# A deformable convolution's last tap summed on VectorE, and a new order of the engines' steps

## What is computed

```python
for oy in (0.0, 1.0):
    for ox in (0.0, 1.0):
        yy, xx = (y0 + oy, x0 + ox)
        wgt = (1.0 - jnp.abs(ys - yy)) * (1.0 - jnp.abs(xs - xx))
        ...
        out = out + jnp.where(valid, wgt, 0.0)[..., None] * g
...
return jnp.einsum('npkgc,npkg->npgc', out, mk)
...
d = _dcn_core(v, off, mask) @ op_w.T
z = d @ cv2_w.T
```

## Time and profile before

| | us |
|---|---|
| median of 3 runs | 918.97 (918.94 to 920.76) |
| profiled execution | 918.25 |
| its span, first to last instruction | 916.4 |
| sampling, first product to last row sum | 52.9 to 421.9 |
| attention, first gather to last scatter | 622.6 to 772.7 |

### The profile page before, as it was taken

How to read it: one execution, slowest core, us unless ns; L and a number is a source line. 1 busy time by engine, 2 the same in 40 slices (tenths; PEclk the granted TensorE clock), 3 DMA queues, 4 the chain that set the end, 5 groups by cost and what they waited for, 6 DMA issues and landing times.

```text
span 916.4 us, 10354 instructions
## 1 busy us (share of the span) xinstructions
PE 599.2 (65%) x3032; PEld 446.3 (49%) x3032; DVE 538.9 (59%) x1018; ACT 322.0 (35%) x536; POOL 465.7 (51%) x364
## 2 busy tenths in 40 slices
PE   1566878787878787761288888873867771656511
PEld 0445556565656565640265665652656661445300
DVE  3257878797969796962366566552564654444411
ACT  2435352525252525100154554551232320433400
POOL 0058988899989998996100000004575733000075
PEclk9967575758585858555599999986686875677755
DMA  9463526565556562600445455410010101445311
GB/s 359 145 151 80 144 58 150 167 146 171 142 163 151 168 145 68 151 0 23 153 129 160 151 159 171 147 45 15 12 30 23 30 15 33 128 129 138 100 33 37
DMA packets 67013, 101.22 MB, mean 110 GB/s; under 512 B 25742, under 2 KB 45198, under 8 KB 66958
## 3 DMA queue, kind: packets, MB, share of 16 engines
q1 hardware_dynamic: 62416, 93.07, 35.7%
q0 software_dynamic: 4096, 6.30, 2.6%
q10 hardware_dynamic: 446, 1.20, 0.4%
HBM read 37.67 MB, written 25.10 MB: 68 GB/s over the span
## 4 chain that ended last, share of the span: by engine, by line
PE 32%; DVE 19%; issue 18%; POOL 13%; ACT 9%; SPq 5%; DMA 4%; POOLq 0%; DVEq 0%; ACTq 0%
DVE sb_prod L1085 6%; POOL sb_yg L1382 5%; POOL xs L1363 5%; PE ps_pa L479 4%; PE ps_t L514 4%; PE ps_c L472 3%; PE ps_t L581 2%; PE ps_pb L599 2%; DVE sb_hats L1160 2%; DVE sb_hats L1071 2%; ACT sb_hats L859 2%; PE ps_t L582 1%; PE ps_t L590 1%; PE ps_t L589 1%; PE ps_c L499 1%
## 5 line engine op out<-in xcount | busy, mean ns | idle before, releaser
L1351 POOL TENSOR_TENSOR sb_acc<-sb_acc,sb_prod 128x1024 f32<-128x1024 f32 x128 | 300.2, 2376 | 12.0 <-DVE sb_prod L1085 11.7
L1382 POOL DMA_INDIRECT sb_yg<-ys,sb_jdx x64 | 61.4, 959 | 295.3 <-DMA ys<-sb_yt 277.3
L514 PE MATMUL ps_t<-sb_vbd,sb_hx 128*128 128x256 f32 x576 | 139.9, 391 | 69.9 <-DVE sb_prod L1085 57.8
L1085 DVE TENSOR_TENSOR sb_prod<-ps_t,sb_hy 128x1024 f32<-128x1024 f32 x128 | 153.6, 1216 | 41.7 <-PE ps_t L514 31.9
L514 PEld LDWEIGHTS ps_t<-sb_vbd,sb_hx 128*128 128x128 f32 x576 | 110.1, 267 | 100.2 <-DVE sb_prod L1085 70.1
L1363 POOL DMA_INDIRECT xs<-sb_xr,sb_idx x64 | 64.4, 1007 | 25.4 <-issue 15.8
L1213 DVE TENSOR_TENSOR sb_hid<-ps_t,sb_hid 114x512 f32<-114x512 f32 x69 | 46.4, 686 | 46.3 <-ACT sb_hid L880 41.0
L499 PE MATMUL ps_c<-sb_dwT,sb_omx 128*128 128x256 f32 x144 | 53.5, 527 | 14.8 <-DVE sb_hats L1071 10.2
L880 ACT ACTIVATE sb_hid<-ps_t 114x512 f32<-114x512 f32 x69 | 41.2, 599 | 48.0 <-PE ps_t L582 47.9
L499 PEld LDWEIGHTS ps_c<-sb_dwT,sb_omx 128*128 128x128 f32 x144 | 34.9, 259 | 23.3 <-issue 17.4
L479 PE MATMUL ps_pa<-sb_ypad,sb_diag 128*64 128x256 f32 x96 | 40.8, 599 | 8.2 <-ACT sb_yrep L781 8.2
(11 more groups left out here) (253 smaller groups left out, 1294.2 us busy)
## 6 DMA issues: line engine op xcount, KB each, us to landing
sb_hx<-sb_hats SPq DMA_DIRECT2D x384, 96.0 KB, 2.2
xs<-sb_x3t SPq DMA_DIRECT2D x32, 512.0 KB, 6.1
sb_acc<-in_wcat SPq DMA_DIRECT2D x16, 876.0 KB, 4.5
sb_yrep<-in_wcat SPq DMA_DIRECT2D x7, 876.0 KB, 4.5
sb_nt<-xs SPq DMA_DIRECT2D x32, 128.0 KB, 2.1
sb_acc<-in_ucat SPq DMA_DIRECT2D x22, 160.0 KB, 2.4
sb_xt<-xs SPq DMA_DIRECT2D x23, 128.0 KB, 2.2
ys<-sb_yt SPq DMA_DIRECT2D x16, 128.0 KB, 2.4
```

The source lines that it names most:

```text
L514: last = mm(tb[u % 2][:, j * 256:(j + 1) * 256], hx[q % 3][:, j, o:o + P], vbd[n % 2][:, j * 256:(j + 1) * 256], start=True, stop=True)
L1085: v.tensor_tensor(o.rearrange("p (g c q) -> p g c q", g=G, q=H), tb[u % 2][:, :].rearrange("p (g c q) -> p g c q", g=G, q=H), w, ALU.mult) ...
L1351: g.tensor_tensor(acc[n % 2][:, t, :], acc[n % 2][:, t, :], prod[a % 3][:, :], ALU.add).then_inc(s_pool_acc, 1)
L1382: g.indirect_dma_start(out=yg[b][:, t, z, :], out_offset=None, in_=ys[0:NJT[m] * TILE, :], in_offset=bass.IndirectOffsetOnAxis(ap=jdx[m][: ...
```

## The change

The ninth tap (k = 8) is no longer added by GpSimd. VectorE makes its product as before, and right behind it sums that buffer over the 16 rows into a new tile `dlast` (one reduction for each half of the pixels). GpSimd adds taps 1 to 7: 14 adds per image. `sampled` on TensorE no longer transposes `dsum`; it multiplies `dsum` and `dlast` by the identity into the same PSUM region, two accumulating products for each half. The buffers' counts follow: `added` says how many adds must be done before a buffer is free. TensorE now waits for `s_dve_last` too. All five strings of `WEAVE` differ.

```diff
-ADDS = UNITS - TT
+ADDS = UNITS - 2 * TT
...
+        dlast = sb("dlast", [P, TT, C])
...
             def sampled(n):
                 pe.wait_ge(s_dve_dr, n + 1)
+                pe.wait_ge(s_dve_last, n + 1)
                 if n:
                     pe.wait_ge(s_dve_rk[0], 2 * n)
-                to_channels(pb, dsum).then_inc(s_pe_dt, 1)
+                for t in range(TT):
+                    mm(pb[0:C, t * P:(t + 1) * P], dsum[:, t, :], ident[:, :], start=True, stop=False)
+                    last = mm(pb[0:C, t * P:(t + 1) * P], dlast[:, t, :], ident[:, :], start=False, stop=True)
+                last.then_inc(s_pe_dt, 1)
...
+            def added(a):
+                n, i = divmod(a, UNITS - TT)
+                return ADDS * n + min(i + 1, ADDS)
+
             def tap(n, k, t):
                 u = UNITS * n + k * TT + t
-                a = ADDS * n + (k - 1) * TT + t
+                a = (UNITS - TT) * n + (k - 1) * TT + t
...
-                        dve.wait_ge(s_pool_acc, a - 2)
+                        dve.wait_ge(s_pool_acc, added(a - 3))
...
+                if k == K - 1:
+                    dve.wait_ge(s_dve_p, u + 1)
+                    if n:
+                        dve.wait_ge(s_pe_dt, n)
+                    last = v.tensor_reduce(dlast[:, t, :], o.rearrange("p (c r) -> p c r", r=H), AX, ALU.add)
+                    if t == TT - 1:
+                        last.then_inc(s_dve_last, 1)
...
             def tap(n, k, t):
-                if k == 0:
+                if k in (0, K - 1):
                     return
...
-                g.tensor_tensor(acc[n % 2][:, t, :], acc[n % 2][:, t, :], prod[a % 3][:, :], ALU.add).then_inc(s_pool_acc, 1)
+                g.tensor_tensor(acc[n % 2][:, t, :], acc[n % 2][:, t, :], prod[(a + TT * n) % 3][:, :], ALU.add).then_inc(s_pool_acc, 1)
...
-        zzzzzzzzaa aaaapaaazz paaazzpaaa zzpaaazzpp ppaaaaaaxx xxxdxdxdxd xdxdxdxdxd xdxdxdxdxd xdxdxdxdxd xddddxxxxx dxxddxdxxx
+        zzzzzzzzaa aaaapaaapz zaaapzzaaa pzzaaapppp zzaaaaaaxx xxxdxdxdxd xdxdxdxdxd xdxdxdxdxd xdxdxdxdxd xddddxxxxx dxxddxdxxx
```

33 lines of the change are left out of this document (17 added, 16 removed).

## The result

The changed kernel takes **953.8 us** (median of 4 runs, 950.4 to 954.8), the kernel before in the same comparison 919.9 us (918.9 to 921.5): ratio 1.0359, 95% interval 1.0335 to 1.0383, slower by 34 us. The forecast was 930.5 us, range 904 to 942. The direction was right, the size was not, and the time lies above the range.

The account below looks back on a forecast made before the run. It took GpSimd's adds and TensorE's convolution chain with VectorE behind it as about equally late. From 918.25 us, +5.6 (sampling), -4.6 (stage end), +10.6 (attention) and 0.7 to the median gave 930.5 us, range 904 to 942.

Parts of the forecast that it names:

- part 1: Sampling stage, GpSimd: two adds fewer, 4.7 us an image; its loop of about 43.3 us would allow a 2.6 us gain.
- rival A: Sampling stage: GpSimd keeps the pace, so the period falls to 43.3 us; 906.8 us, 12 in 100.
- part 2: Sampling stage, VectorE: two reductions of 1.21 us add 2.4 us an image, with no wait for their product.
- part 3: Sampling stage: VectorE idles 7.0 us against 8.3, period 46.65 us, 0.8 us more per image, +5.6 us in all.
- The two waits at the core: Sampling stage, VectorE: waits on TensorE for the transposed x1, 3.6 us, and for the logits, 2.9 us.
- part 4: Sampling stage, TensorE: four joining products replace two transposes, +0.7 to +1.6 us an image, taken as covered and charged 0.
- the slow bound: Sampling stage: upper bound of 48.0 us for the period, with all TensorE work at the lower clock.
- part 5: End of the sampling stage: two late GpSimd adds of 2.31 us go, -4.6 us.
- part 6: Attention stage's new order: one more scatter left after the gathers (63.0 us), 17.0 us of GpSimd waits among them; +10.6 us.
- B: Sampling stage: TensorE's high clock from the start of depthwise, period 44.6 us; 915.9 us, 14 in 100.
- C: Attention stage: the new order costs nothing, GpSimd's waiting among the gathers stays at 6.4 us; 920 us, 12 in 100.
- E: Sampling stage: TensorE's low clock throughout, period 48.0 us, and attention +14.6 us; 943.6 us, 9 in 100.

Follow-up runs that it names:

- relief_only: Kernel before in its order, with 14 GpSimd adds an image, the ninth tap left out of the sum and two transposes kept; 915.0 us, ratio 0.9951.
- new_order_relief: Changed kernel with the attention order of before, without ninth-tap row sums, two transposes instead of joining products; 916.7 us, ratio 0.9973 to the kernel before.
- last_only: Kernel before in its order, with the changed ninth-tap work in the last image alone (126 adds instead of 128); 913.6 us, ratio 0.9939.
- code_old_order: Changed kernel's work with the whole order of steps of the kernel before; 929.7 us, ratio 1.0118 to the kernel before.
- early_slots: early_rank with VectorE's slot sum and ScalarE's slot copy of images 2 to 4 also ahead of key maxima and exponentials; 957.2 us.
- late_scatter: old_attention with GpSimd's scatter descriptors of images 0 to 3 moved behind the hits of the next image; 933.0 us.
- early_rank: Changed kernel with TensorE's rank products of images 2 to 4 moved earlier and VectorE's rank ahead of the key maxima; 958.9 us.
- combined: old_attention with x1 ahead of depthwise products, z and column products behind a tap, and GpSimd's scatter behind the next image's hits; 925.7 us.
- x1_first: old_attention with x1's transposes ahead of the depthwise products for images 1 to 4, its dependent steps and logits moved up; 925.4 us.
- early_x1: Kernel before with summed-tap transposes, z, x1 and its norm moved earlier for images 1 to 5; 930.1 us, ratio 1.0109.
- old_attention: Changed kernel with the attention stage's order of before, sampling order as changed; 935.5 us, ratio 1.0171 to the kernel before.

## Why the prediction went wrong

- **GpSimd's relief (part 1)**: its price was right (4.7 us of GpSimd's time a period forecast, 4.5 measured) and so was that VectorE with its waits was the later of the two. relief_only shows that the relief gives nothing in the period. The 43.3 us of rival A came in neither order.
- **Reductions (part 2)**: priced at 2.42 us a period, 2.2 measured over the regular images. That they stand on the path was right: VectorE's work adds to the period nearly one to one.
- **VectorE's idle time (part 3), the step that failed most.** The two waits at the core were forecast at 3.6 and 2.9 us and are 4.49 and 2.10, together 6.6 against 6.5: the sum is right by luck, since the two errors cancel. The third term, "some 0.5 us" ahead of the third tap, is 0.46 + 1.07 + 1.02 = 2.55 us in three places: z, then the norm's transposes with the `cv1` product, then the last column products with the transposes of x stand between taps. The first of them was priced right; the other two had no term. And the busy time was summed from durations at their old places: the copy (+1.20) and the mask (+0.66) grew since adds of GpSimd now stand beside them. 46.65 + 2.05 (short waits) + 1.9 (longer operations) + 0.1 (core waits) = 50.7, and 51.2 was measured; 0.5 is small gaps that I don't place. A smaller slip: 46.65 was built on an image of 45.50 us and compared with a mean of 45.9, so the step from its own image was +1.15 a period and not +0.8, 8 us in seven and not 5.6. The rule that two inputs in SBUF meet GpSimd's reads could have been read off: 1.74 us for a mask of 128x32 is long, and I did not ask why.
- **Joining products (part 4)**, charged at 0: they cost 0.7 us a period in the old order, the low end of the range. In the changed order no run parts them from the reductions; the two together add 2.5 us to VectorE's busy time there and 0.9 us to its idle time (new_order_relief against the changed kernel), and the reductions themselves are 2.44 of it. Most of the 0.9 us is the wait for x1, 4.49 instead of 3.27 us, at a granted clock of 0.67 instead of 0.79. TensorE stands 2.77 us for the row sums, makes the joining products in 1.9 us and only then z and the third tap; VectorE's wait ahead of that tap is 0.46 us and 0.19 without them, so the cover was nearly there, but not full. The forecast called an uncovered price "inside the slow bound", but the bound of 48.0 had no term for it.
- **End of the stage (part 5)**: -3.1 instead of -4.6. Two adds go, but VectorE's last products and reductions now end last. With the same work last_only reached -4.4 and code_old_order -4.0, so about 1 us of the gain was lost to the changed order.
- **Attention (part 6)**: up to the last gather the sum holds. From the end of the gather of image 3 (677.1) to that of image 7 (739.3) it is 62.2 us, and 45.2 + 17.0 was forecast; that it fits so closely is in part luck, since the single waits are off by up to 1.3 us. They were 2.2 (forecast 3.1), 3.7 (4.1), 0.7 (1.5), 3.0 (2.4), 5.4 (4.1) and 1.8 (1.8). The tail is 68.2 us instead of 63.0: the scatter behind the last gather ended 9.6 us on instead of 7.9, the next 17.4 instead of 14.3, and the last three took 13.75 each, as forecast. The term that is off most is the second scatter: I took its step from the old order, where image 7's queries, keys and values stood behind the rank of image 4, while in the changed order they stand ahead of it. That this makes the 3.1 us is not shown: with rank and slots moved ahead of them (early_slots) the step is 18.3 us. The first four gathers took 0.9 us longer.
- **Rivals.** B wanted the high clock from the start of the depthwise products: the granted clock of an image fell from 0.73 to 0.67. The depthwise products took 5.12 us at a granted clock of 0.54, close to the forecast's 5.0 and not the rival's 3.2. In one image of late_scatter they took 3.91 and VectorE's wait was shorter by the same 1.21 us, so the rival's way from the clock to the wait exists; what it had wrong is when the high level comes. The rule of the Trainium skill on which it leaned ("TensorE: Matmul & The Clock Gate", What's actually happening) is not refuted, since TensorE still stood idle now and then ahead of these products (0.56 us ahead of the tap at 263.75), but the time that I drew from it was wrong. C (the attention order is free) is out by 17 to 18 us. E, the low clock throughout at 943.6, came nearest, 10 us short; its price for the period, 48.0, had neither the joining products nor the longer copy in it.
- **The range** ended at 942: it took in waits of the attention stage up to 22 us and stopped just short of the low-clock case (943.6); the longer operations and the joining products were in neither. Both signs that I named for being wrong, a period below 45 and scatters faster than every 13 us, looked for a kernel faster than forecast; neither came in the regular images (only image 6, in its own order, has 44.3). An order that is new as a whole has more unknown terms than one: one for each operation that gets a new neighbour.

## What to carry to other kernels

Before an engine is relieved, ask what the period does without its work at no other price: here a kernel that only leaves the adds out shows that there was nothing to gain but at the end of the stage, where the change then paid in one image alone. When steps move, price each moved operation at its new neighbours, above all those of VectorE with two inputs in SBUF beside GpSimd's work, and count every product that stands between two taps. A wait found in a list of waits is a link of a chain: taking it away moved it elsewhere in early_rank, early_slots and combined.

## What was new on the hardware

- The same VectorE copy of 128x1024 with two inputs in SBUF takes 1.28 us beside GpSimd's descriptors, mostly 2.48 beside its adds, and 4.13 when an add starts 0.67 us into it. Each time it ends 1.1 us after an add ends, and that need not be the add that ran when it started: in new_order_relief one copy sat through the rest of one add and the whole of the next, to 1.08 us after the train of five ended (348.42 + 11.66 = 360.08):

```profile
356.12 5.04 DVE L1046 SCALAR_TENSOR_TENSOR sb_vbd<-sb_vh,sb_wide,sb_vm 128x1024 fp32r<-128x1024 f32 x1
```

```profile
348.42 11.66 POOL L1356 TENSOR_TENSOR sb_acc<-sb_acc,sb_prod 128x1024 f32<-128x1024 f32 x5
```

- The one-hot mask of 128x32 takes 0.19 us at the end of the stage, where no adds run, and up to 2.42 beside them; that it is the same cause is argued from its place beside the adds (0.60 to 0.75 us where x1_first moved it, 0.25 to 0.37 in combined), not tested alone. Reductions with one input take 1.21 to 1.22 us in all kernels.
- Descriptors don't hinder the copy, but the copy hinders them: one that starts within a copy ends 0.84 us after it and takes 1.25 us (before, at 308.28) to 1.83 us (late_scatter, at 179.66) instead of 0.96.
- An early start doesn't always protect the copy: in three meetings of early_x1 it had started 0.26 to 0.67 us ahead of the add and was ended after it; with 0.93 us of lead it was not held up. The Trainium skill ("SBUF — State Buffer", SBUF: two separate sides) says that whichever starts first keeps the ports for its whole instruction; by the starts that the profile shows, three of these four meetings differ from it. Whether the profile's start is the moment at which the ports are taken, no run tells.
- TensorE's granted clock in one image of the same work went from 0.67 to 0.74 when only a scatter of GpSimd was moved (late_scatter), and from 0.75 down to 0.68 when z, the column products and that scatter were moved (combined). The mean clock of whole runs goes the same way: 0.733 to 0.745 in the four runs of late_scatter against 0.717 to 0.730 of old_attention, 0.723 to 0.738 in combined against 0.741 to 0.745 in x1_first. Its busy time for the image followed, 39.6 to 36.4 us and 36.8 to 38.0. An order is thus not priced by durations of another order, not even on the engine whose steps stay.
